# Two heads' scores in one bank, one weighing group per narrow step, and other edits at the ends of the program

## The chip, the cores and the metric

The kernel runs on one core of a Trainium2 chip. The metric is the device time of one execution in microseconds (us). Three runs of the kernel before took 2128.0, 2130.17 and 2129.55 us; the median is 2129.55.

## The reference

The input is x with 2 batches of 1024 tokens and 512 features, in float32. Four residual blocks follow one another:

```
x = x + attention_a(layernorm(x));  x = x + ffn(layernorm(x))
x = x + attention_b(layernorm(x));  x = x + ffn(layernorm(x))
attention: 16 heads of 32, qkv with bias, scores * 32**-0.5, causal mask, softmax, values, output projection with bias
ffn: (silu(h @ w_gate.T) * (h @ w_up.T)) @ w_down.T, hidden size 2048; both ffn blocks share their weights
```

## The kernel before, in words

The program runs four iterations: 2 batches by 2 layers, each an attention and an ffn. Weights and activations are split into a high and a low part (`hi`, `lo`), and each product is three matmuls of type fp32r (`three`, lines 1165 to 1167). Every engine has its own written-out order of work, and semaphores tie them together.

The attention of an iteration is cut into 8 units. Unit u is a group of four heads (u // 2) and a chunk of 512 query tokens (u % 2). `key_tiles(u)` is 4 for an even unit and 8 for an odd one: a unit steps over key tiles j of 128 keys. In each step TensorE computes four transposed score tiles (`scores_t`, line 1256), one for each head, keys by queries, into banks 0 and 1 in turn; ScalarE takes each with one exp into `prob` (`exps`, line 713); in the last four steps of a unit GpSimd masks the diagonal tile of all four heads at once (`mask_probs`, line 605); and TensorE weighs the step before (`weigh`, line 1278): eight matmuls of a 128x32 stationary for the values (the trace has two for each head) and eight for the sums of the exps, into banks 2 and 3. In the last four steps the tiles narrow: `off` leaves 512, 384, 256 and 128 query columns. The order within a step is scores of heads 0 and 1, values, scores of heads 2 and 3, sums, with a place ("point") behind each of the four.

At the points stand the first-pass scores of the next units (`scores`, line 1232, called s1), whose row maxima VectorE takes (`maximum`, line 908), the transposes of the maxima (`mt`, line 1239), and in unit 7 the output projections (`op`) and transposes (`ln2`). `points(u)` computes the places. The maxima, split and negated, go by two small DMAs (`nm_hi`, `nm_lo`) into two more rows of the query stack, and the first transposed score of a unit waits for them.

A unit begins with a head: the q and k projections of unit u + 2 (24 matmuls) in halves, the last weighing of unit u - 1 (`weigh_last`), the scores of step 0, and for units 0, 1, 3 and 5 some early s1 (`BETWEEN`: 2, 1, 2, 1). For the odd units the transpose of their own maxima comes late, in their own head (`MAX_LATE`). ScalarE's order in a head is: evacuate the last unit, the high part of q, the four exps of step 0, the high part of k (line 702). VectorE's order is written out too: the low part of k (line 897) comes ahead of the sixth early s1 (`LO_BEFORE`), and the eight parts of a reciprocal of 512 columns (line 929) lie one behind each s1 from the seventh on.

At the start, VectorE first sets 6144 ones in two rows of the key stacks (line 842), then takes the statistics of the first four token tiles; GpSimd splits the weights of slot 0, then computes the inverse deviation (line 598), then splits slots 1 and 2; VectorE normalises four tiles (line 871), TensorE transposes them, and the value products begin once both value slots are split. At the end, SP stores each of the last batch's eight token tiles and, two tiles later, loads x again into the same place; nothing reads the last four of these.

Of the kernel before, what the change touches and what calls it, by code (L numbers as in the profile page):

```python
# [96 lines left out]

def key_tiles(u):
    return CT * (unit(u)[1] + 1)
# [22 lines left out]

def points(u):

    if u == UNITS - 1:
        return [6, 8, 10, 12, 21, 25]
    if u == UNITS - 2:
        return [0, 2, 4, 6, 10]
    n = len(beside(u)) - sum(BETWEEN.get(u, ()))
    first = FIRST[unit(u)[1]]  # L130
    return [first + i * (4 * (key_tiles(u) - 1) - TAIL - first) // n for i in range(n)]
# [31 lines left out]
LO_BEFORE = {0: (2, 5), 1: (2, 5), 3: (2, 5), 5: (2, 5)}  # L163
RECIPS_FROM = 6
# [17 lines left out]
def block_kernel(nc, x_in, attn_w, ffn_w, qk_bias, row_bias, out):  # L182
    with ExitStack() as ctx:
# [3 lines left out]
        def sem(name):  # L187
# [79 lines left out]
            sem("diff_step"), sem("diff_hi_done"), sem("diff_ready"), sem("s_step"))  # L267

# [142 lines left out]
        def _(sp):  # L411
# [45 lines left out]
            with sp.Fori(0, BATCH) as b:  # L457
# [31 lines left out]
            for s in x_loaded:  # L489
                sp.wait_ge(s, 16 * CT * (BATCH + 1))  # L490
# [7 lines left out]
        def _(pool):  # L498
# [130 lines left out]
            split_weights(0, 0)  # L629
# [49 lines left out]
        def _(act):  # L679
# [11 lines left out]
            def iteration(it):  # L691
# [13 lines left out]
                def exps(u, j, heads):  # L705
                    step = J_BASE[u] + j
                    off = max(0, j - CT * unit(u)[1]) * P
                    if step >= 2:
                        act.wait_ge(pv_done, it * KEY_STEPS + step - 1)
                    for h in heads:  # L710
                        n = GH * step + h
                        act.wait_ge(s2_full, it * S2_STEPS + n + 1)
                        act.activation(prob[:, step % 2, h, off:], bank[n % 2][:, off:], ACT.Exp,  # L713
# [119 lines left out]
            load_table(ACT.Exp)  # L833
            xt_to_hi(0, ("ln1", 0))
# [6 lines left out]
        def _(dve):  # L841
            dve.memset(k_stack[3 * HEAD:3 * HEAD + 2, 1:, :, :].bitcast(F32), 1.0).then_inc(ones_ready, 1)
# [302 lines left out]
        def _(pe):  # L1145
# [13 lines left out]
            def iteration(it):  # L1159
# [15 lines left out]
                def value_part(t, k):  # L1175


                    if k == 0:
# [7 lines left out]
                        pe.wait_ge(w_split, it * SLOTS + V_SLOTS[1] + 1)  # L1186
# [11 lines left out]
                def project(u, w, half):  # L1198

                    g, c = unit(u)  # L1200
                    if half == 0:
# [6 lines left out]
                        if w == 0:  # L1208
# [4 lines left out]
                             for k in range(half * KT // 2, (half + 1) * KT // 2)]  # L1213
                    ins = three(projected(u, w), terms, half == 0, half == 1)
                    if half == 1:
# [26 lines left out]
                def scores_t(u, j, h):  # L1242
# [10 lines left out]
                    if n >= 2:  # L1253
                        pe.wait_ge(prob_ready, it * S2_STEPS + n - 1)
                    rows = slice(0, 3 * HEAD + 2)
                    pe.matmul(bank[n % 2][:, off:], k_stack[rows, keys_of(u, j // CT), h, j % CT * P:(j % CT + 1) * P],  # L1256
# [152 lines left out]
                def project_whole(u, w):  # L1409
                    for half in range(2):  # L1410
                        project(u, w, half)
# [20 lines left out]
                for u in range(UNITS):  # L1432
# [8 lines left out]
                    def between(quarter):  # L1441

                        nonlocal early
                        if u in BETWEEN:
                            for what, *which in beside(u)[early:early + BETWEEN[u][quarter]]:
                                run[what](*which)
                            early += BETWEEN[u][quarter]

                    if u + 2 < UNITS:
                        project(u + 2, 0, 0)  # L1450
                        if u in MAX_LATE:
                            transpose_max(u)
                        weigh_last()
                        between(0)
                        project(u + 2, 0, 1)
                        between(1)
                        scores_t(u, 0, 0)
                        scores_t(u, 0, 1)
                        project(u + 2, 1, 0)
                        between(2)  # L1460
                        scores_t(u, 0, 2)
                        scores_t(u, 0, 3)
                        project(u + 2, 1, 1)
                        between(3)
# [12 lines left out]
                    for j in range(1, key_tiles(u)):  # L1477
                        for half, what in enumerate(("values", "sums")):
                            for own in range(2):
                                if own == 0:  # L1480
                                    scores_t(u, j, 2 * half)
                                    scores_t(u, j, 2 * half + 1)
                                else:
                                    weigh(u, j - 1, what)
                                for (name, *which), at in zip(beside(u)[early:], points(u)):
                                    if at == point and (name != "mt" or which[0] not in MAX_LATE):
                                        run[name](*which)
                                point += 1
# [75 lines left out]
```

## Time and profile before

| | |
|---|---|
| median of 3 runs | 2129.55 us |
| the profiled execution's own time | 2128.06 us |
| its span, first to last instruction | 2126.3 us |
| TensorE busy in the span | 2058.0 us, 97% |
| VectorE, ScalarE, GpSimd busy | 57%, 33%, 47% |
| mean granted TensorE clock | 0.996 |
| VectorE: low part of k (line 897); row maximum (line 908), mean of all | 0.75 us; 0.75 us |
| weight load of TensorE, mean (lines 1256 and 1232) | 0.19 us |
| iteration 2, first transposed score of unit 2 to that of unit 3 | 1175.84 to 1193.58: 17.7 us |
| iteration 2, unit 7, first to last transposed score | 1295.69 to 1327.63: 31.9 us |

The profiled execution took 1.76 us more than its span and 1.49 us less than the median. Its busy time of TensorE counts a matmul from its start to a modelled end, and neighbouring matmuls overlap: a row of 512 columns lasts 390 ns, and the next one starts after some 230 ns. So the pace is read from the starts of the rows, not from their lengths.

### The profile page before, as it was taken

What the parts mean: (1) busy time and instruction counts of PE and PEld (TensorE: products, weight loads), DVE (VectorE), ACT (ScalarE), POOL (GpSimd) and SP (SyncE); (2) the same over time, 40 slices, a digit from 0 to 9 for tenths busy, and PEclk for the clock granted to TensorE, in tenths of its full rate; (3) what the DMA queues carried; (4) which work ended last, traced back from release to release, by engine and by line L of the source; (5) the groups of instructions that cost most, each with busy time, mean ns of one, the idle gap of its engine ahead of it and who ended that gap; (6) DMA issues with size and microseconds to landing.
All of it is one profiled execution on the core that took longest, in us unless ns stands there. A gap on an engine that the chain in (4) does not pass through costs nothing.

```text
span 2126.3 us, 35275 instructions
## 1 busy us (share of the span) xinstructions
PE 2058.0 (97%) x10816; PEld 1442.8 (68%) x10816; DVE 1210.5 (57%) x2452; ACT 698.6 (33%) x1348; POOL 998.0 (47%) x776
## 2 busy tenths in 40 slices
PE   6999999999999999999989999999999999999997
PEld 5555478888755547888765554888887554588886
DVE  6766554455676645544557664555456666444454
ACT  1344432231144443222114444222221444422221
POOL 3323249863312425975331242697533223379752
PEclk9999999999999999999999999999999999999999
DMA  4433101111323200111243320111113232111112
GB/s 130 99 80 82 32 30 50 60 60 40 81 72 81 71 31 30 63 50 58 70 131 72 81 71 32 40 60 50 50 41 83 68 81 71 41 40 60 50 60 89
DMA packets 59756, 135.18 MB, mean 64 GB/s; under 512 B 10784, under 2 KB 11808, under 8 KB 59552
## 3 DMA queue, kind: packets, MB, share of 16 engines
q1 hardware_dynamic: 59552, 132.71, 22.1%
q8 instruction: 98, 1.61, 0.3%
q14 instruction: 106, 0.87, 0.1%
HBM read 77.62 MB, written 4.19 MB: 38 GB/s over the span
## 4 chain that ended last, share of the span: by engine, by line
PE 89%; DVE 3%; issue 3%; ACT 2%; DMA 1%; POOL 1%; SPq 0%; DVEq 0%; POOLq 0%; ACTq 0%
PE bank L1278 13%; PE bank L1165 11%; PE bank L1167 11%; PE bank L1166 11%; PE ring L1165 10%; PE ring L1166 9%; PE ring L1167 9%; PE ring L1232 8%; PE bank L1256 7%; PE ring L1156 1%; ACT prob L713 1%; DMA area<-nm_lo 1%; DVE xn L908 1%; POOL prob L605 1%; DMA x<-x_in 0%
## 5 line engine op out<-in xcount | busy, mean ns | idle before, releaser
L713 ACT ACTIVATE prob<-bank 128x512 f32<-128x512 f32 (+3 forms) x768 | 335.0, 489 | 342.0 <-PE bank L1256 341.2
L908 DVE CUSTOM_DVE_ANT_0 xn<-ring,mask_row 128x128 bf16<-128x128 f32 (+7 forms) x512 | 374.8, 750 | 104.8 <-PE ring L1232 97.8
L605 POOL TENSOR_SCALAR_AFFINE_SELECT prob<-prob 128x512 f32<-128x512 f32 x128 | 83.9, 655 | 567.5 <-ACT prob L713 567.5
L528 POOL TENSOR_SCALAR area<-w_stage 128x1024 fp32r<-128x1024 f32 x131 | 149.8, 1143 | 381.0 <-PE bank L1167 206.7
L530 POOL TENSOR_TENSOR area<-w_stage,area 128x1024 fp32r<-128x1024 f32 x131 | 313.8, 2396 | 10.9
L967 DVE TENSOR_TENSOR x<-x,bank 128x512 f32<-128x512 f32 x256 | 170.8, 685 | 233.2 <-PE bank L1167 233.2
L1165 PE MATMUL ring<-xt_hi,area 128*128 128x512 f32 x688 | 273.8, 398 | 5.2 <-DVE xt_lo L880 2.8
L1166 PE MATMUL ring<-xt_lo,area 128*128 128x512 f32 x688 | 269.4, 392 | 0.0
L1167 PE MATMUL ring<-xt_hi,area 128*128 128x512 f32 x688 | 268.9, 391 | 0.0
L1232 PE MATMUL ring<-area 96*128 96x512 f32 (+3 forms) x768 | 238.8, 372 | 9.5 <-DVE row_max L908 8.5
L1232 PEld LDWEIGHTS ring<-area 96*128 96x128 f32 x768 | 131.0, 188 | 151.0 <-DVE row_max L908 94.6
L1256 PE MATMUL bank<-area 98*128 98x512 f32 (+3 forms) x768 | 225.3, 372 | 7.9 <-DMA area<-nm_lo 4.0
L1256 PEld LDWEIGHTS bank<-area 98*128 98x128 f32 x768 | 125.5, 190 | 122.4 <-ACT prob L713 96.2
L1165 PE MATMUL bank<-area 128*128 128x512 f32 x512 | 200.6, 392 | 2.7 <-DVE area L1035 2.7
L1167 PE MATMUL bank<-area 128*128 128x512 f32 x512 | 199.5, 390 | 0.0
L1166 PE MATMUL bank<-area 128*128 128x512 f32 x512 | 199.5, 390 | 0.0
L1278 PE MATMUL bank<-prob,v 128*32 128x512 f32 (+3 forms) x1536 | 164.4, 500 | 9.1 <-POOL prob L605 7.3
L1278 PE MATMUL bank<-prob,ones 128*32 128x512 f32 (+3 forms) x1536 | 163.2, 497 | 0.0
L1165 PEld LDWEIGHTS ring<-xt_hi,area 128*128 128x128 f32 x688 | 129.6, 188 | 44.2 <-issue 9.8
L1167 PEld LDWEIGHTS ring<-xt_hi,area 128*128 128x128 f32 x688 | 129.7, 189 | 27.7
L1166 PEld LDWEIGHTS ring<-xt_lo,area 128*128 128x128 f32 x688 | 129.9, 189 | 25.5
L929 DVE RECIPROCAL recip<-recip 128x64 f32<-128x64 f32 x256 | 123.8, 522 | 15.0 <-ACT attn L723 15.0
(144 smaller groups left out, 3231.8 us busy)
## 6 DMA issues: line engine op xcount, KB each, us to landing
w_stage<-ffn_w SPq DMA_DIRECT2D x96, 512.0 KB, 3.2
area<-kq_parts SPq DMA_DIRECT2D x336, 128.0 KB, 2.4
w_stage<-attn_w SPq DMA_DIRECT2D x35, 512.0 KB, 3.3
x<-x_in SPq DMA_DIRECT2D x24, 256.0 KB, 3.8
area<-attn SPq DMA_DIRECT2D x48, 128.0 KB, 2.3
out<-x SPq DMA_DIRECT2D x16, 256.0 KB, 2.2
bias_rows<-row_bias SPq DMA_DIRECT2D x10, 256.0 KB, 4.2
area<-nm_hi SPq DMA_DIRECT2D x32, 8.0 KB, 1.8
```

The source lines that it names most:

```text
L528: pool.tensor_scalar(hi, src, 1.0, 0.0, ALU.mult, ALU.add).then_inc(w_hi_done, 1)
L530: pool.tensor_tensor(lo, src, hi.bitcast(F32), ALU.subtract).then_inc(w_split, 1)
L713: act.activation(prob[:, step % 2, h, off:], bank[n % 2][:, off:], ACT.Exp, scale=SCALE).then_inc(prob_ready, 1)
L908: dve.tensor_tensor_reduce(out=sum_out[:, RING[name] % 2, 0:keys], in0=src[:, 0:keys], in1=mask_row[:, TOKENS - keys:], scale=1.0, scalar= ...
L929: dve.reciprocal(recip[:, cols], recip[:, cols]).then_inc(recip_done, 1)
L967: dve.tensor_tensor(x[:, t, :], x[:, t, :], row_bank(s, n)[:, :], ALU.add).then_inc(rows_drained, 1)
L1165: pe.matmul(dst, ah, bh, start=first and k == 0, stop=False, skip_group_check=more)
L1166: pe.matmul(dst, ah, bl, start=False, stop=False, skip_group_check=more)
L1167: ins = pe.matmul(dst, al, bh, start=False, stop=last and k == n - 1, skip_group_check=more)
L1232: ins = pe.matmul(buffer_of(("s1", u, s))[:, kc, 0:n], q, k_stack[0:3 * HEAD, keys_of(u, kc), h, 0:n], start=True, stop=True)
L1256: pe.matmul(bank[n % 2][:, off:], k_stack[rows, keys_of(u, j // CT), h, j % CT * P:(j % CT + 1) * P], q_stack[rows, q_buffer(u), h, off:], ...
L1278: ins = pe.matmul(dst[rows, off:], a, prob[:, step % 2, h, off:], start=j == 0, stop=j == key_tiles(u) - 1, tile_position=(0, h * HEAD))
```

## The change

- `narrow(u, j)` is true in the last two key tiles of a unit (256 and 128 columns). There, `scores_at` puts heads 0 and 1 side by side in bank 0 and heads 2 and 3 in bank 1, ScalarE takes two heads with one exp, and `STEP_PARTS` orders the step as scores of heads 0 and 1, scores of heads 2 and 3, values and sums in one group, nothing. Each of the four parts still has a point behind it. `scores_t` waits for the exps that last read its bank.
- `POINTS` gives the places by hand. `UNIT_START` writes out the head: for even units it is the order of before; for odd units half of the k projection comes ahead of the scores of heads 0 and 1, a quarter behind them and the last quarter behind those of heads 2 and 3. `project` takes a range of its four parts.
- GpSimd sets the ones at the start, and only waits for the four normalised tiles before it subtracts for the low parts of the two value slots; their high parts are made by ScalarE. A value product waits for the slot that it reads.
- SP no longer loads x into the last four tiles of the last batch; the program waits for the stores instead. The batch loop of SP is unrolled.

```diff
+def narrow(u, j):
+    return j >= key_tiles(u) - 2
...
+POINTS = {0: (0, 1, 2, 3, 4, 6, 8, 10, 11), 2: (0, 3, 5, 9, 9), 4: (0, 3, 5, 9, 9),1: (0, 1, 2, 3, 4, 5, 6, 7, 8, 9, 10, 11, 12, 13, 14, 15, 17, 18, 19, 21, 22, 25, 26),6: (0, 2, 4, 5, 10), 7: (4, 8, 10, 12, 21, 25)}
...
+    return POINTS[u if u in POINTS else unit(u)[1]]
...
+STEP_PARTS = (((0,), ("values",), (1,), ("sums",)), ((0,), (1,), ("values", "sums"), ()))
...
+    (("project", 0, range(0, 2)),
+     ("max",),
+     ("last",),
+     ("s1", 2),
+     ("project", 0, range(2, 4)),
+     ("s1", 1),
+     ("project", 1, range(0, 2)),
+     ("scores", 0, 1),
+     ("project", 1, range(2, 3)),
+     ("s1", 2),
+     ("scores", 2, 3),
+     ("project", 1, range(3, 4)),
+     ("s1", 1)))
...
+            if narrow(u, j):
+                n = CHUNK - off
+                return bank[h // 2][:, h % 2 * n:(h % 2 + count) * n]
+            return bank[h % 2][:, off:]
...
-                        if n >= AFTER_STORE:
+                        if n >= AFTER_STORE and not (b == BATCH - 1 and c):
...
+            pool.memset(k_stack[3 * HEAD:3 * HEAD + 2, 1:, :, :].bitcast(F32), 1.0).then_inc(ones_ready, 1)
+            pool.wait_ge(ones_ready, 1)
             inverse_deviation(0, 0, 0)
-            for i in range(1, AHEAD):
+            wait_alone(pool, xn_ready, CT)
+            for i in V_SLOTS:
+                hi, lo = w_part(i, slice(0, SLOT))
+                wait_alone(pool, w_hi_done, i + 1)
+                pool.tensor_tensor(lo, w_stage[:, i, :], hi.bitcast(F32), ALU.subtract).then_inc(w_split, 1)
+            for i in range(len(V_SLOTS), AHEAD):
                 split_weights(0, i)
...
+                    if narrow(u, j):
+                        for h in heads[::2]:
+                            act.wait_ge(s2_full, it * S2_STEPS + GH * step + h + 2)
+                            src = scores_at(u, j, h, 2).rearrange("p (h n) -> p h n", h=2)
+                            act.activation(prob[:, step % 2, h:h + 2, off:], src, ACT.Exp,
+                                           scale=SCALE).then_inc(prob_ready, 2)
+                        return
...
+            for i in V_SLOTS:
+                act.wait_ge(w_loaded[i], 16)
+                act.activation(w_part(i, slice(0, SLOT))[0], w_stage[:, i, :], ACT.Copy).then_inc(w_hi_done, 1)
...
+                    if k % 2 == 0:
+                        pe.wait_ge(w_split, it * SLOTS + V_SLOTS[k // 2] + 1)
...
+                    if narrow(u, j):
+                        pe.wait_ge(prob_ready, it * S2_STEPS + n - h - GH + (GH if h >= 2 else 2 if narrow(u, j - 1) else 3))
+                    elif j == 0 and h < 2 and n >= 2:
+                        pe.wait_ge(prob_ready, it * S2_STEPS + n - h - GH + 2 + 2 * h)
...
```

## Rows read from the trace of the kernel before

**Rows 1.** The page, part 1: busy time, share and instructions of each engine.
```profile
PE 2058.0 (97%) x10816; PEld 1442.8 (68%) x10816; DVE 1210.5 (57%) x2452; ACT 698.6 (33%) x1348; POOL 998.0 (47%) x776
```

**Rows 2.** Waits of TensorE over the span: total us, times, longest.
```profile
PE bank L1278 <- POOL prob L605: 7.3, 20, 0.6
```

**Rows 3.** Timeline of TensorE: start us, us, engine, line, operation (unit 1, iteration 2).
```profile
1171.61 0.64 PE L1278 MATMUL bank<-prob,ones 128*32 128x256 f32 x8
1172.18 0.50 PE L1165 MATMUL ring<-xt_hi,area 128*128 128x512 f32 x1
1172.52 0.40 PE L1166 MATMUL ring<-xt_lo,area 128*128 128x512 f32 x1
1172.75 0.39 PE L1167 MATMUL ring<-xt_hi,area 128*128 128x512 f32 x1
...
1173.44 0.39 PE L1167 MATMUL ring<-xt_hi,area 128*128 128x512 f32 x1
1173.76 0.43 PE L1278 MATMUL bank<-prob,v 128*32 128x128 f32 x8
1174.00 0.40 PE L1278 MATMUL bank<-prob,ones 128*32 128x128 f32 x8
1174.33 0.51 PE L1165 MATMUL ring<-xt_hi,area 128*128 128x512 f32 x1
```

**Rows 4.** Timeline of TensorE, end of unit 7, iteration 3; bracket: idle before.
```profile
1842.68 0.85 PE L1278 MATMUL bank<-prob,v 128*32 128x384 f32 x8 [0.38 <-POOL prob L605]
...
1849.21 0.43 PE L1278 MATMUL bank<-prob,v 128*32 128x128 f32 x8 [0.62 <-POOL prob L605]
```

**Rows 5.** Timeline at the heads of units 1, 3 and 5, iteration 2.
```profile
1140.68 0.72 PE L1256 MATMUL bank<-area 98*128 98x512 f32 x2 [0.68 <-DMA area<-nm_lo]
...
1193.29 0.45 PE L1232 MATMUL ring<-area 96*128 96x384 f32 x1 [0.59 <-DVE row_max L908]
...
1246.84 0.73 PE L1256 MATMUL bank<-area 98*128 98x512 f32 x2 [0.34 <-DMA area<-nm_lo]
```

**Rows 6.** Timeline of ScalarE at the head of unit 1.
```profile
1143.38 1.08 ACT L713 ACTIVATE prob<-bank 128x512 f32<-128x512 f32 x2 [1.09 <-PE bank L1256]
1144.99 0.69 ACT L702 ACTIVATE kq_parts<-ring,bias_qk 128x512 fp32r<-128x512 f32 x1 [0.53 <-PE ring L1167]
```

**Rows 7.** Tile x, first 3 us: transfers issued and their time to landing.
```profile
L448 SPq DMA_DIRECT2D x<-x_in x4: 390/426/432, 0.8 to 2.2; - x4
DMA to landing us min/median/max: 2.7/3.2/4.3
```

**Rows 8.** Timeline of VectorE, the start of the program.
```profile
2.16 5.18 DVE L842 MEMSET area<- 2x6144 f32 x1 [2.16 <-issue]
7.45 2.44 DVE L848 BATCH_NORM_STATS2 stats<-x 128x6 f32<-128x512 f32 x4
12.57 3.75 DVE L871 TENSOR_SCALAR xn<-x,mean_var,rstd 128x512 f32<-128x512 f32 x2 [1.14 <-POOL rstd L598]
...
31.24 1.00 DVE L871 TENSOR_SCALAR xn<-x,mean_var,rstd 128x512 f32<-128x512 f32 x2 [0.49 <-POOL rstd L598]
```

**Rows 9.** Timeline of TensorE, the start.
```profile
16.46 1.94 PE L1156 MATMUL ring<-ident,xn 128*128 128x128 f32 x8 [16.46 <-DVE xn L871]
...
21.71 0.78 PE L1165 MATMUL ring<-area,xt_hi 128*128 128x512 f32 x1
```

**Rows 10.** Groups of GpSimd by line: busy us, mean ns.
```profile
L530 POOL TENSOR_TENSOR area<-w_stage,area 128x1024 fp32r<-128x1024 f32 x131 | 313.8, 2396 | 10.9
L671 POOL MEMSET area<- 2x6144 f32 x4 | 20.9, 5229 | 0.5
```

**Rows 11.** Timeline of the SP queue, end of the program.
```profile
2119.34 0.33 SPq L484 DMA_DIRECT2D out<-x  x1
2119.83 3.15 SPq L488 DMA_DIRECT2D x<-x_in  x3
```

**Rows 12.** Busy time and granted clock in one stretch of unit 7, iteration 1.
```profile
769.30:772.70 3.40, 3.40 (x14) 0.71 (x10) 0.00 (x0) 1.54 (x4) 3.14 (x4) 0.50 0.00 0
```

More of the change, by code:

```diff
@@ L163 @@
 LO_BEFORE = {0: (2, 5), 1: (2, 5), 3: (2, 5), 5: (2, 5)}
+STEP_PARTS = (((0,), ("values",), (1,), ("sums",)), ((0,), (1,), ("values", "sums"), ()))
+UNIT_START = (
+    (("project", 0, range(0, 2)),
[7 more added lines that the diff above has]
+     ("scores", 2, 3),
+     ("project", 1, range(2, 4)),
+     ("s1", 1)),
+    (("project", 0, range(0, 2)),
+     ("max",),
+     ("last",),
+     ("s1", 2),
+     ("project", 0, range(2, 4)),
+     ("s1", 1),
+     ("project", 1, range(0, 2)),
+     ("scores", 0, 1),
+     ("project", 1, range(2, 3)),
+     ("s1", 2),
+     ("scores", 2, 3),
+     ("project", 1, range(3, 4)),
+     ("s1", 1)))
 RECIPS_FROM = 6
@@ L456, in _ @@
                 load_weights(i, None, attn_w[0])
-            with sp.Fori(0, BATCH) as b:
+            for b in range(BATCH):
                 with sp.Fori(0, LAYERS) as layer:
@@ L1212, in project @@
                     terms = [(*w_part(QK_SLOT0 + g, slice((2 * k + w) * P, (2 * k + w + 1) * P)), *xt_part(k, cols))
-                             for k in range(half * KT // 2, (half + 1) * KT // 2)]
-                    ins = three(projected(u, w), terms, half == 0, half == 1)
-                    if half == 1:
+                             for k in ks]
+                    ins = three(projected(u, w), terms, ks[0] == 0, ks[-1] == KT - 1)
+                    if ks[-1] == KT - 1:
                         ins.then_inc(side_full if u in SIDE_UNITS else ring_full, 1)
@@ L1409, in project_whole @@
                 def project_whole(u, w):
-                    for half in range(2):
-                        project(u, w, half)
+                    project(u, w, range(KT))
                 for t in range(CT - 1):
@@ L1439, in iteration, with between @@
                     early = 0
-                    def between(quarter):
+                    def between(count):
                         nonlocal early
[L1444 to L1447, printed above, removed]
+                        for what, *which in beside(u)[early:early + count]:
+                            run[what](*which)
+                        early += count
                     if u + 2 < UNITS:
[L1450 to L1464, printed above, removed]
+                        for what, *which in UNIT_START[unit(u)[1]]:
+                            if what == "project":
+                                project(u + 2, *which)
+                            elif what == "max" and u in MAX_LATE:
+                                transpose_max(u)
+                            elif what == "last":
+                                weigh_last()
+                            elif what == "scores":
+                                for h in which:
+                                    scores_t(u, 0, h)
+                            elif what == "s1" and u in BETWEEN:
+                                between(*which)
                     else:
@@ L1477, in iteration @@
                     for j in range(1, key_tiles(u)):
[L1478 to L1482, printed above, removed]
+                        for part in STEP_PARTS[narrow(u, j)]:
+                            for what in part:
+                                if what in (0, 1):
+                                    scores_t(u, j, 2 * what)
+                                    scores_t(u, j, 2 * what + 1)
                                 else:
                                     weigh(u, j - 1, what)
[L1485 to L1488, printed above, removed]
+                            for (name, *which), at in zip(beside(u)[early:], points(u)):
+                                if at == point and (name != "mt" or which[0] not in MAX_LATE):
+                                    run[name](*which)
+                            point += 1
                 weigh(UNITS - 1, key_tiles(UNITS - 1) - 1, "values")
```

32 lines of the change are left out of this document (13 added, 19 removed).

## The prediction

> **What bounds the kernel now.** I read the page's busy shares first, then TensorE's waits, then the timeline at the places that the change touches. TensorE is busy for 97% of the span and no other engine for more than 57% [rows 1], so time goes down only where TensorE does less, waits less, or starts earlier, or where the program ends sooner after it. The reader is to see that little of the gain can be in recorded waits: those on GpSimd's mask, the largest inside the iterations, are 7.3 us in all [rows 2]. What the change removes is mostly inside "busy", and only the starts of the rows show it.
>
> **1. Merged weighing.** Take the starts in [rows 3]. Plain products follow each other in 0.23 us (1172.52 to 1172.75). A product followed by a weighing group takes 0.32 (1173.44 to 1173.76): 0.09 to go in. The 128-column values go over to the sums in 0.24, the sums to a product in 0.33: 0.09 to come out, and none between values and sums. The first product behind a group takes 0.34 (1172.18 to 1172.52) where others take 0.23: 0.11 more, which I read as a weight load that could not run ahead. So a separate group costs 0.18 us for the two changes, and up to 0.29 with the load.
> The new order takes out one group in each narrow step: 2 steps x 8 units x 4 iterations = 64. Unit 7 is in part 2; 56 are left. Where s1 still stands beside the scores the whole 0.29 goes; where four short score tiles now come together, weight loads bind them and part of it stays. Ends: 56 x 0.18 = 10.1 and 56 x 0.29 = 16.2 us. I take 0.26, nearer the upper end since in the odd units s1 stands at four of the eight narrow points: 14.6 us. The paired exps take time from ScalarE alone, which is off the path; a pair must wait for its second head's matmul, but its reader comes a whole group later.
> The Trainium skill, "TensorEngine Tiling (Array Packing)", section "Tiling Modes", says that a change of tiling mode drains the engine. It names only the drain, so by it alone this part would be the lower end, some 4.5 us less than I take; the 0.34 behind a group in [rows 3] says that there is more to a change than the two drains.
>
> **2. The end of unit 7.** Nothing but transposes fills its last steps, and three values groups stand for the mask; the first and last idle 0.38 and 0.62 us [rows 4]. Before, the exps of heads 2 and 3 come between values and sums, and the mask behind them is late. In the new order they come a whole group (1.0 to 1.4 us) and eight transposes earlier, so mask and exps are done. Walking the new order from 1841.79: two pairs of 256 columns 0.45, transposes 0.9, values and sums of 384 columns 4 x 0.33 + 0.2; two pairs of 128 columns 0.5, transposes 0.9, 8 groups of four matmuls of 256 columns at 0.22, then the last weighing without a stall, 0.55. The first product of the output projection stands at about 1848.1, where the last weighing of before [rows 4] ends at 1849.2 + 0.57 = 1849.8. That is 1.7 us, both merges counted: 6.8 in four iterations. Ends: the merges alone, 0.5 each, 2.0; and 1.9 each, 7.6.
>
> **3. Heads of the odd units.** The first transposed score of unit 1 idles 0.68 us for the maxima's DMA and that of unit 5 0.34; in unit 3 the wait is before, on VectorE (0.59), and stays [rows 5]. By starts the two are worth 0.8 and 0.6. Six products (1.36 us) now stand ahead of those scores, so these stalls go. But what is late next? ScalarE must still do two exps (1.08) and the high part of k (0.69) [rows 6], then VectorE the low part (0.75) and one row maximum (mean 0.75, for one of 256 columns some 0.4; both in the table above), before the eighth s1 has its buffer; with the scores of heads 2 and 3 followed by only three products instead of six, and an s1 at each of points 0 and 1 where only point 1 had one, TensorE reaches that s1 some 0.4 us too early, in all three units. 4 x (0.8 + 0.6 + 0.05) = 5.8 gained, 12 x 0.4 = 4.8 lost. I take a gain of 1.0; ends: a gain of 5.8, a loss of 5.
> The other moved points cost nothing in my account: in units 1, 3 and 5 all s1 come earlier or at the same distance, so that VectorE has more room at the narrow end. The output projection in unit 7 moves from point 6 to 4; its input was split about 0.9 us before that point, and if it were late the price would be under 1 us an iteration.
>
> **4. The start.** Four tiles of x are issued by 2.2 and the last takes up to 4.3 [rows 7]: in place at 6.5. VectorE starts on them only at 7.45, behind its 5.18 us of ones, which go to GpSimd (5.23 there [rows 10]) and end by 8.1. So statistics start 0.9 earlier. The inverse deviation then finds GpSimd idle instead of in a subtraction (2.4 [rows 10]). And two normalised tiles take 3.75 us [rows 8] while GpSimd splits weights, but 1.00 when it does not. My walk: statistics 6.55 to 9.6, inverse deviation to 10.7, four tiles to 12.7, high and low parts of the first pair to 16.3, when the first value product starts; it was at 21.71 [rows 9]. Low part of slot 0 is there at 15.2, of slot 1 at 17.6, both in time. 5.4 us earlier; TensorE runs the first stretch at the slower pace and has more of its products in it, for which I take off 0.4. Gain 5.0, ends 4.0 and 5.4; slot 2 comes at 22.2 where it is read at some 26, so the lead is kept.
> The Trainium skill, "SBUF — State Buffer", section "Who interferes with whom", says that GpSimd shares a port pair with some VectorE instructions and that the one issued second blocks. The 3.75 against 1.00 agrees. By the same rule the ones, if still being written when VectorE's first such instruction is issued, would hold it; they end a microsecond earlier, so the sum stays.
>
> **5. The end.** The last store is issued at 2119.34, held by the order of stores and loads, and three loads end the program [rows 11]: the span ends 2126.3. Without them the last store goes out at about 2118.6, lands 2.2 to 3.2 later and the program ends 0.5 behind it: 2121.3 to 2122.3. Gain 4.6, ends 4.0 and 5.0.
>
> **Sum.** 14.6 + 6.8 + 1.0 + 5.0 + 4.6 = 32.0. The profiled execution's own time is 2128.06: 2096.1. The median of the runs stood 1.5 above it; the profiled execution itself holds stretches at the lower of TensorE's two levels (granted 0.50, that is 1.2 GHz, in 3.4 us of unit 7 [rows 12]), and such things vary by run. I forecast 2097.5.
>
> **Rivals.**
> A. *Only the drains go.* Scores of narrow tiles come in fours, and their weight loads take back what the group's end gave. For it: a weight load lasts 0.19 us (the table), and 128 columns stream in a quarter of the 0.23 that 512 take. Against it: pairs of 128 columns were so bound before. Then 10.1 + 4.0 - 4.0 + 5.0 + 4.6 = 19.7: 2109.9 on the median's scale. The skill's rule on draining points here. Chance 0.14.
> B. *Heads pay fully and nothing new is late.* If VectorE's lead is longer than my walk says, part 3 gives 5.8; with the upper ends of part 1 the sum is 38.4: 2091. For it: VectorE is busy for 57% only. Chance 0.18.
> C. *The start is handed back.* The projections wait for slot 2, or VectorE for the second four tiles, whose times hang on loads and not on TensorE. Then 27: 2102.5. Against it: 4 us of slack above. Chance 0.08.
> D. *Slower.* The heads of the odd units become a chain: scores of heads 2 and 3, two exps, high part of k, low part of k, maximum, 0.3 + 1.08 + 0.69 + 0.75 + 0.4 = 3.2 us, with nothing beside it. 12 x 3.2 = 38 against 31: 2136. It decides from 2.6 us a head on. Against it: between those scores and the s1 that waits stand some 2.6 us of TensorE's own work. Chance 0.04.
> The forecast has 0.56.
>
> **Range and chances.** The lower ends of all parts give 2129.5 - 15 = 2114, the upper ones 2129.5 - 40 = 2089.5. I give 2089 to 2109, which takes in A's edge and B. A change of under 0.2% (4 us) could not be told from none here. Slower by more: D, 0.04. Within: 0.03, where A, C and half of D come together. Faster: 0.93.
>
> **What would show it.** Right: in the last two steps of a unit the weighing rows stand as 16 matmuls in a line, and a unit 2 or 4 takes 0.5 us less from first score to first score (17.7 before, the table); no mask waits at the end of unit 7, which is 1.7 us shorter; first transposes near 11.9 and first value product near 16.3; the last transfer is a store. Wrong: s1 waits on VectorE at the second point of units 1, 3 and 5 longer than 0.5 us, pairs of narrow scores start more than 0.3 us apart, or a new wait on the weights of slot 2 at some 26 us. The forecast falls if the iterations after the first give less than 3 us each.

## The result, and the profile after

The changed kernel takes 2079.24 us (median of 5 runs, 2076.52 to 2083.13) against 2129.55: a ratio of 0.9765, 95% interval 0.9749 to 0.9781. The forecast was 2097.5 with a range of 2089 to 2109, so the sign was right and the gain of 50 us was larger than the range allows.

The profiled execution took 2079.24 us itself, with a span of 2077.5 us against 2126.3. The page of the changed kernel gives each engine's busy us, share of the span and instructions:

```profile
PE 2033.5 (98%) x10816; PEld 1444.8 (70%) x10816; DVE 1197.3 (58%) x2451; ACT 688.0 (33%) x1222; POOL 999.9 (48%) x775
```

Its waits of TensorE: total us, times, longest.

```profile
PE ring L1286 <- DVE row_max L961: 5.5, 16, 0.6
...
PE bank L1314 <- ACT prob L764: 3.7, 12, 0.5
...
PE bank L1336 <- POOL prob L643: 0.7, 4, 0.2
```

TensorE's instructions are as many as before [rows 1] and 24.5 us of its busy time are gone; the other half of the 48.8 us by which the span is shorter was idle time. GpSimd's mask is waited for 4 times in place of 20 [rows 2], and the maxima's DMA has no row at all; in the kernel before it had this one:

```profile
PE bank L1256 <- DMA area<-nm_lo: 4.0, 8, 0.7
```

Where the 48.8 us lie, from the starts of rows in the two traces (first and last transposed score of each iteration, last matmul, end of span):

| stretch | before | after | gain | forecast |
|---|---|---|---|---|
| start of the span to the first transposed score | 68.80 | 61.80 | 7.0 | 5.0 |
| four attentions, first to last transposed score | 835.3 | 797.2 | 38.1 | |
| last transposed score to the next iteration's first, three times, and to the last matmul | 1210.7 | 1212.4 | -1.7 | |
| the two rows above, parts 1 to 3 | | | 36.4 | 22.4 |
| last matmul to the end of the span | 11.47 | 6.06 | 5.4 | 4.6 |

Every part gave more than its term, and the iterations hold 14 of the missing 17 us. An attention without a stretch at half clock takes 198.9 to 199.0 us in place of 208.4 to 208.5.

The narrow steps at the end of unit 1, iteration 2, in the trace of the changed kernel (start us, us, engine, line, operation), which answer to [rows 3]:

```profile
1104.89 0.34 PE L1314 MATMUL bank<-area 98*128 98x128 f32 x2
...
1105.52 0.34 PE L1314 MATMUL bank<-area 98*128 98x128 f32 x2
1105.79 0.64 PE L1336 MATMUL bank<-prob,v 128*32 128x256 f32 x8
1106.25 0.61 PE L1336 MATMUL bank<-prob,ones 128*32 128x256 f32 x8
1106.79 0.74 PE L1286 MATMUL ring<-area 96*128 96x512 f32 x2
```

Values and sums are one line of 16 matmuls, one change in and one out. The end of unit 7, which answers to [rows 4]: no bracket, thus no wait, at the last two steps, and the last weighing 0.9 us behind the first of its group.

```profile
1803.34 0.66 PE L1314 MATMUL bank<-area 98*128 98x128 f32 x4
1803.84 1.06 PE L1209 MATMUL ring<-ident,attn 128*128 128x128 f32 x8
1804.83 0.64 PE L1336 MATMUL bank<-prob,v 128*32 128x256 f32 x8
1805.28 0.61 PE L1336 MATMUL bank<-prob,ones 128*32 128x256 f32 x8
1805.72 0.40 PE L1336 MATMUL bank<-prob,v 128*32 128x128 f32 x8
```

The head of unit 1, which answers to the first row of [rows 5]: six more products stand between s1 and the first transposed score, and no wait is recorded.

```profile
1111.66 0.34 PE L1286 MATMUL ring<-area 96*128 96x384 f32 x1
1111.83 0.40 PE L1218 MATMUL ring<-xt_hi,area 128*128 128x512 f32 x1
...
1112.98 0.39 PE L1220 MATMUL ring<-xt_hi,area 128*128 128x512 f32 x1
1113.21 0.63 PE L1314 MATMUL bank<-area 98*128 98x512 f32 x2
...
1116.00 0.79 PE L1314 MATMUL bank<-area 98*128 98x512 f32 x2
1116.62 0.34 PE L1286 MATMUL ring<-area 96*128 96x384 f32 x1
1116.90 1.07 PE L1336 MATMUL bank<-prob,v 128*32 128x512 f32 x8
1117.99 0.50 PE L1286 MATMUL ring<-area 96*128 96x512 f32 x1
```

The start on VectorE, against [rows 8]: a pair of normalised tiles takes 1.00 us.

```profile
10.62 1.00 DVE L924 TENSOR_SCALAR xn<-x,mean_var,rstd 128x512 f32<-128x512 f32 x2 [1.22 <-POOL rstd L636]
```

The start on TensorE, against [rows 9]: the first product stands at 16.33, and the next follows in 0.33 and then in 0.23.

```profile
11.77 1.94 PE L1209 MATMUL ring<-ident,xn 128*128 128x128 f32 x8 [11.77 <-DVE xn L924]
13.50 1.80 PE L1209 MATMUL ring<-ident,attn 128*128 128x128 f32 x8
16.33 0.49 PE L1218 MATMUL ring<-area,xt_hi 128*128 128x512 f32 x1 [1.03 <-DVE xt_lo L933]
16.66 0.40 PE L1219 MATMUL ring<-area,xt_hi 128*128 128x512 f32 x1
```

The end on the SP queue, against [rows 11]: four stores, no load behind them.

```profile
2072.73 2.12 SPq L520 DMA_DIRECT2D out<-x  x4
```

Both profiles hold two stretches of 3.4 us at about half the granted clock (1.2 of 2.4 GHz); this is the one of unit 7, iteration 2, as in [rows 12]. That unit took 30.91 us from first to last score where the other three took 29.35, so it cost 1.56 us. Both kernels have one in an attention and one between two attentions, so the difference above holds none.

```profile
1264.50:1267.90 3.40, 3.40 (x14) 0.70 (x10) 0.00 (x0) 1.44 (x3) 3.21 (x4) 0.52 0.00 0
```

### The profile page after: what moved, and what is told of

Same layout as the page of the kernel before. It is cut to its first block, busy times and chain, and to the rows that moved or that the text cites. A ratio compares the mean times of both kernels' runs of the same rounds, so it can differ in the third digit from the quotient of the medians.

```text
span 2077.5 us, 34948 instructions
## 1 busy us (share of the span) xinstructions
PE 2033.5 (98%) x10816; PEld 1444.8 (70%) x10816; DVE 1197.3 (58%) x2451; ACT 688.0 (33%) x1222; POOL 999.9 (48%) x775
## 4 chain that ended last, share of the span: by engine, by line
PE 92%; DVE 3%; issue 3%; ACT 1%; DMA 1%; POOL 0%; DVEq 0%; SPq 0%; POOLq 0%; ACTq 0%
PE bank L1336 13%; PE bank L1218 11%; PE bank L1220 11%; PE bank L1219 10%; PE ring L1218 10%; PE ring L1220 9%; PE ring L1219 9%; PE ring L1286 9%; PE bank L1314 7%; PE ring L1209 1%; DVE xn L961 1%; DMA x<-x_in 0%; ACT prob L764 0%; DVE stats L901 0%; PE ring L1293 0%
## 5 line engine op out<-in xcount | busy, mean ns | idle before, releaser
L764 ACT ACTIVATE prob<-bank 128x512 f32<-128x512 f32 (+1 forms) x512 | 264.4, 570 | 214.8 <-PE bank L1314 214.0
L568 POOL TENSOR_TENSOR area<-w_stage,area 128x1024 fp32r<-128x1024 f32 x129 | 309.1, 2396 | 10.8
L1314 PE MATMUL bank<-area 98*128 98x512 f32 (+3 forms) x768 | 212.1, 365 | 3.9 <-ACT prob L764 3.7
```

Source lines behind the costliest of these rows:

```text
L568: pool.tensor_tensor(lo, src, hi.bitcast(F32), ALU.subtract).then_inc(w_split, 1)
L764: act.activation(prob[:, step % 2, h, off:], scores_at(u, j, h), ACT.Exp, scale=SCALE).then_inc(prob_ready, 1)
L1314: pe.matmul(scores_at(u, j, h), k_stack[rows, keys_of(u, j // CT), h, j % CT * P:(j % CT + 1) * P], q_stack[rows, q_buffer(u), h, off:], s ...
```

## Experiments

"Steps" are the merged order, packing, paired exps and the relaxed waits on exps; "places" is the new table of points. Kernels of one group ran on one chip; each was timed beside the kernel before, whose medians there were 2127.59, 2129.35 and 2129.29 us. The changed kernel was not timed again beside them, so "slower than the changed kernel" compares with the 2079.24 above, whose own kernel before stood at 2129.55. There is one profile of each kernel.

### One part added to the kernel before

**The end alone.**

```diff
-                        if n >= AFTER_STORE:
+                        if n >= AFTER_STORE and not (b == BATCH - 1 and c):
...
```

> The kernel before with the edit at the end of the program alone (no last four loads of x, waits for the stores). If the end is worth what the two traces show between the last matmul and the end of the span (11.4 us before, 6.1 after), the time is 5.4 us below the kernel before. By the term of my forecast it is 4.6, at most 5.0.

2122.58 us, ratio 0.9973 (0.9962 to 0.9985): 5.0 us. Its last matmul starts at 2114.22 and the span ends at 2120.3: 6.1 us, as in the changed kernel.

**The start alone**: ones on GpSimd, value slots split by ScalarE and GpSimd behind the four normalised tiles.

> The kernel before with the edits at the start alone. If the 6.8 us by which the first transposed score comes earlier are the start's own, the time is 6.8 us below the kernel before, and the first value product runs at 0.23 us at once. By my forecast 5.0, at most 5.4, with the first products at 0.43 us for some 4 us.

2121.38 us, ratio 0.9969 (0.9959 to 0.9979): 6.2 us. The first transposed score stands at 63.89, 4.9 us earlier than before and 2.1 later than in the changed kernel. The transposes and the first product stand within 0.05 us of their places there. What differs is the pace behind them; these are its first products:

```profile
16.38 0.79 PE L1174 MATMUL ring<-area,xt_hi 128*128 128x512 f32 x1 [0.92 <-DVE xt_lo L889]
16.96 0.63 PE L1175 MATMUL ring<-area,xt_hi 128*128 128x512 f32 x1
17.39 0.63 PE L1176 MATMUL ring<-area,xt_lo 128*128 128x512 f32 x1
17.81 0.63 PE L1174 MATMUL ring<-area,xt_hi 128*128 128x512 f32 x1
```

They follow each other in 0.43 us, until 20.8, where the changed kernel's follow in 0.23 from the second on. The granted clock is 1.00 in both. So the forecast's 5.0 fits an execution that starts slowly, as the profile of the kernel before does too, and 2.1 of the 7.0 above lie in the pace. The new start comes with both paces: of the eight profiles in this document that hold it, three start at 0.23 and five at 0.43. So I put the 2.1 down to the execution and not to the edit; no kernel was profiled twice to show it.

**The steps alone**, at the old places, with the old heads.

```diff
...
+STEP_PARTS = (((0,), ("values",), (1,), ("sums",)), ((0,), (1,), ("values", "sums"), ()))
```

> The kernel before with the narrow steps alone: paired scores and exps, values and sums in one group, the relaxed waits; the places of s1, the heads, the start and the end are those of before. If one merged group is worth 0.33 us: 64 x 0.33 = 21, and 5 to 9 more for the end of unit 7 and the mask that comes earlier, 26 to 30 us below. By my forecast's terms 14.6 + 6.8 = 21.4, at most 23.8.

2124.4 us, ratio 0.9987 (0.9976 to 0.9997): 3.2 us, where parts 1 and 2 of the forecast sum to 21.4 and I expected 26 to 30. Merging pays here too (the last two steps of unit 2, up to the projection, take 4.57 us where the kernel before takes 5.20), but TensorE now waits for VectorE's maxima 48 times, and for the maxima's DMA longer:

```profile
PE ring L1279 <- DVE row_max L955: 17.9, 48, 0.6
PE bank L1307 <- DMA area<-nm_lo: 6.6, 12, 0.9
```

**The heads alone**: half of the k projection ahead of an odd unit's first scores.

```diff
+     ("project", 1, range(0, 2)),
      ("scores", 0, 1),
-     ("project", 1, range(0, 2)),
+     ("project", 1, range(2, 3)),
      ("s1", 2),
      ("scores", 2, 3),
-     ("project", 1, range(2, 4)),
+     ("project", 1, range(3, 4)),
```

> The kernel before with the heads of units 1, 3 and 5 in the new order alone. If the stalls on the maxima's DMA go and little comes back: 0.8 and 0.6 an iteration less at most 0.3, 4 to 5 us below. By my forecast 1.0 us below (5.8 gained, 4.8 lost on the eighth s1).

2121.29 us, ratio 0.9968 (0.9956 to 0.9979): 6.3 us. An undisturbed attention takes 207.02 us, 1.4 less than before, no waits for the maxima's DMA are left, and waits for row maxima do not grow (7.9 us, 20 times). The forecast's loss of 4.8 at the eighth s1 is not there; but the old places, which this kernel keeps, put no s1 at point 0.

### One part taken out of the changed kernel

**Values and sums apart again** (packing and places stay).

```diff
-STEP_PARTS = (((0,), ("values",), (1,), ("sums",)), ((0,), (1,), ("values", "sums"), ()))
+STEP_PARTS = (((0,), ("values",), (1,), ("sums",)), ((0,), ("values",), (1,), ("sums",)))
```

> The changed kernel with values and sums apart again in the narrow steps (order of before, packed scores and pair exps kept). If a merged group is worth 0.33 us by itself: 64 x 0.33 = 21 slower than the changed kernel, some 25 with the masks at the end of unit 7. By my forecast's price 0.26: 17. If the gain came from the packing or the places of s1 instead: less than 8 slower.

2117.97 us, ratio to before 0.9944 (0.9923 to 0.9965): 38.7 us slower than the changed kernel, more than twice the 14.6 + 2.0 that the groups themselves were to cost and more than the 25 expected. The mask is late:

```profile
PE bank L1336 <- POOL prob L643: 11.0, 28, 0.7
```

That is 10.3 us of it. The last two steps of unit 2 take 5.50 us here, more than the 5.20 of the kernel before: packed scores with the groups apart are worse than either kernel, so the 38.7 is not what merging is worth against the kernel before.

**The old places** under everything else.

```diff
-    return POINTS[u if u in POINTS else unit(u)[1]]
...
+    first = FIRST[unit(u)[1]]
+    return [first + i * (4 * (key_tiles(u) - 1) - TAIL - first) // n for i in range(n)]
```

> The changed kernel with the places of s1 of before. The theory after x3_steps: the merged narrow steps shorten TensorE's part of a step, and with the old places VectorE's row maxima bind there, so that the gain is handed to s1 waits. Then it is 18 to 25 us slower than the changed kernel, with 40 or more waits of s1 on row maxima (16 in the changed kernel). If the places are worth nothing by themselves, as my forecast had it: within 3 us of the changed kernel.

2104.94 us, ratio 0.9888 (0.9869 to 0.9907): 25.7 us slower. Its waits for row maxima are those of the steps alone, 17.9 us in 48 times against 5.5 in 16, which is half of it; the rest stands in no recorded wait. TensorE at the end of unit 1: four s1 stand in a line, and the next ones wait for VectorE, with only packed scores between.

```profile
1118.56 1.03 PE L1292 MATMUL ring<-area 96*128 96x512 f32 x4
1119.42 0.34 PE L1320 MATMUL bank<-area 98*128 98x128 f32 x2
1120.35 0.73 PE L1292 MATMUL ring<-area 96*128 96x512 f32 x2 [0.59 <-DVE row_max L967]
```

**The old heads** under everything else (the diff of the heads, reversed).

> The changed kernel with the odd heads in the order of before. If the head is worth in company what it was alone (5.7 us by its trace): 5 to 7 slower than the changed kernel, with eight waits on the maxima's DMA back. If VectorE is later there with the new places: more, 8 to 10. By my forecast 1.0.

2092.3 us, ratio 0.9827 (0.9808 to 0.9847): 13.1 us slower, twice what the heads gave alone and more than the 10 expected. The maxima's DMA is waited for 12 times:

```profile
PE bank L1313 <- DMA area<-nm_lo: 9.9, 12, 1.3
```

**No packing**: the merged order stays (by a function of its own), heads take banks 0 and 1 in turn again, with one exp each, and each score waits again for the exp of the score two before it.

```diff
 def narrow(u, j):
-    return j >= key_tiles(u) - 2
+    return False
...
-                        for part in STEP_PARTS[narrow(u, j)]:
+                        for part in STEP_PARTS[short(u, j)]:
```

> The changed kernel with the merged order in the narrow steps, but each head's scores in banks 0 and 1 in turn and one exp for each head. The scores of heads 2 and 3 must then wait for the exps of heads 0 and 1 of their own step. If packing is what lets the group be merged, 128 such waits of 0.2 to 0.4 us, partly behind an s1: 15 to 35 us slower than the changed kernel. If packing is only ScalarE's saving and off the path: within 3 us.

2116.68 us, ratio 0.9941 (0.9923 to 0.996): 37.4 us slower. The scores of heads 2 and 3 now follow those of heads 0 and 1 into the same banks and must wait for their exps:

```profile
PE bank L1317 <- ACT prob L769: 19.4, 64, 0.5
```

In the changed kernel such waits are 3.7 us in 12 times, so the record names 15.7 of the 37.4. Packing is what lets the merged order pay, not an extra of ScalarE's.

### Steps and places together, places alone, and two more

The eight kernels left open whether steps and places by themselves account for the iterations.

> The kernel before with two edits together, the narrow steps (packed, merged, relaxed waits) and the new places, but its old heads, start and end. Theory (steps and places need each other): alone the steps gave 5 us and the places are worth 22 us only where the steps are merged, so the two together give what the changed kernel keeps beyond its heads, start and end: 26 to 31 us, 2099 to 2104, attention of an iteration about 202 us (208.4 before), waits for row maxima down from 17.9 us to about 8, none on GpSimd's mask over 1 us in all. Rival of the prediction's account (places cost and give nothing, steps 14.6 + 6.8 = 21.4): about 2108, and attention 203 us. Rival that effects only add up by single edits (5 us from the steps, nothing from places): 2124.

2107.62 us, ratio 0.99 (0.988 to 0.992): 21.7 us. An undisturbed attention takes 202.1 us, as the theory had it, but part is handed on behind its last score, and four stretches at half clock stand in the profile where the kernel before has two. The theory of 2099 to 2104 failed; the forecast's sum for parts 1 and 2, 21.4, is met. The heads, not the steps, hold what is missing. TensorE at the heads of units 1, 3 and 5 of iteration 2 here:

```profile
1128.00 0.34 PE L1273 MATMUL ring<-area 96*128 96x384 f32 x1
1129.38 0.72 PE L1301 MATMUL bank<-area 98*128 98x512 f32 x2 [1.04 <-DMA area<-nm_lo]
...
1181.34 0.72 PE L1301 MATMUL bank<-area 98*128 98x512 f32 x2 [0.83 <-DMA area<-nm_lo]
...
1233.17 0.72 PE L1301 MATMUL bank<-area 98*128 98x512 f32 x2 [0.34 <-DMA area<-nm_lo]
```

Against [rows 5], unit 1's wait has grown from 0.68 to 1.04, and unit 3 has one of 0.83 where it had none.

**The places alone** in the kernel before.

> The kernel before with the new places alone; steps, heads, start and end as before. Theory (the places pay only beside merged steps): with values and sums apart, the places that the merged steps leave between scores and weighing fall elsewhere, the narrow steps lose cover, and waits for exps or the mask grow: between 3 us faster and 10 us slower than before, 2126 to 2140, attention 208 to 211 us an iteration. Rival (the places themselves carry the 22 us, by giving VectorE room): 2107, attention 203 us. Rival (places are worth nothing by themselves, as in the prediction): within 2 us of before.

2134.34 us, ratio 1.0026 (1.0016 to 1.0036): 5.1 us slower. Waits for the mask grow from 7.3 us [rows 2]:

```profile
PE bank L1275 <- POOL prob L602: 10.2, 32, 0.6
```

The four corners, as gain against the kernel before on the same chip:

| | old places | new places |
|---|---|---|
| old steps | 0 | -5.1 |
| new steps | 3.2 | 21.7 |

21.7 - 3.2 + 5.1 = 23.6 us belong to neither alone. So it is only beside the steps that the places cost nothing, as the forecast had it.

**GpSimd subtracts without waiting** for the normalised tiles.

```diff
-            wait_alone(pool, xn_ready, CT)
```

> The changed kernel, in which GpSimd no longer waits for the four normalised tiles before it subtracts for the low parts of the value slots. Theory (GpSimd's subtractions slow VectorE's normalise, 3.75 us for two tiles in the kernel before against 1.00 without them): the normalise rows take 2 to 4 us a pair again, the first product stands 1 to 4 us later than 16.33, and the products behind it start at the slower pace for longer if the transposes have gaps; first transposed score at 64 to 67 (62.0 in the changed kernel), median 2081 to 2085. Rival (no contention between the two here; the 3.75 came from something else): normalise rows 1.0 us, the same first score or up to 1 us earlier, median 2078 to 2080.

2086.93 us, ratio 0.9805 (0.9786 to 0.9823): 7.7 us slower than the changed kernel. VectorE at the start of this kernel:

```profile
11.08 5.04 DVE L923 TENSOR_SCALAR xn<-x,mean_var,rstd 128x512 f32<-128x512 f32 x2 [1.22 <-POOL rstd L636]
16.03 0.99 DVE L923 TENSOR_SCALAR attn<-x,mean_var,rstd 128x512 f32<-128x512 f32 x2
```

GpSimd, the same stretch:

```profile
11.01 4.82 POOL L674 TENSOR_TENSOR area<-w_stage,area 128x1024 fp32r<-128x1024 f32 x2
```

While GpSimd works (11.01 to 15.83) VectorE needs 5.04 us for two tiles, behind it 0.99. The first theory holds, but its price was too low: the first product stands at 20.82, 4.5 us later, where at most 4 were expected, and the median is above the 2085 of its upper end. The pace behind the product is 0.23 in both, and the first score stands at 66.26, 4.5 us later too. Most of the other 2.6 us of span lie in the change from the first batch to the second (321.77 against 318.85 us from score to score); that stretch varies from 317.0 to 322.3 over the kernels here, and what sets it was not looked into.

**The merged order in every step**, packing still in the last two alone.

```diff
-STEP_PARTS = (((0,), ("values",), (1,), ("sums",)), ((0,), (1,), ("values", "sums"), ()))
+STEP_PARTS = 2 * (((0,), (1,), ("values", "sums"), ()),)
```

> The changed kernel with the merged order (scores of heads 0 and 1, scores of heads 2 and 3, values and sums as one group) in every key tile of every unit; packing and paired exps stay in the last two. It takes out one more weighing group in 32 steps an iteration, 128 in all. Theory 1 (a removed group is worth 0.33 us also in wide steps, where exps have a step's time): 128 x 0.2 to 0.33 = 26 to 42 us faster than the changed kernel, 2037 to 2053. Theory 2 (in wide steps banks are the limit: scores of the next step need the bank whose exp comes last, with nothing between the two pairs of scores but s1 places, so TensorE waits for ScalarE's exps at 0.54 us each): waits on exps of 0.3 to 1.0 us a step, 10 to 60 us slower, 2090 to 2140. I hold theory 2, since each bank serves two heads in turn and four exps of 512 columns take 2.2 us.

2152.04 us, ratio 1.0111 (1.0091 to 1.0131): 72.8 us slower than the changed kernel, though 128 groups fewer change in and out. I held the second theory; its place was right, its upper bound too low. Waits on exps and on row maxima:

```profile
PE bank L1314 <- ACT prob L764: 23.5, 65, 0.6
PE ring L1286 <- DVE row_max L961: 22.9, 52, 1.0
```

Against the changed kernel's 3.7 and 5.5 these two rows hold 37 of the 72.8 us.

## Why the prediction was wrong

**Part 3, the heads, is the step that failed: 1.0 forecast, 13.4 found.** The steps and places together take 23.0 us off the iterations and the heads, added last, 13.4: four attentions take 833.8 us before, 808.4 with steps and places and 795.7 in the changed kernel, each without its half-clock stretches (one, three and one at 1.55 us), and the stretches between them and to the last matmul give 2.3 back and take 0.7 off again. The medians agree: 13.1 for taking the heads out. Added first, the heads give 6.3, also above the 5.8 of the term's upper end; the 7 us between the two figures belong to heads, steps and places together. Two things were wrong in the term.

*The loss.* "TensorE reaches that s1 some 0.4 us too early, in all three units" was to cost 4.8 us. ScalarE's and VectorE's chain is as long as I had it: from the scores of heads 2 and 3 (1114.67) to the end of the maximum that, by the forecast, the eighth s1 needs it takes 3.26 us, where rival D has 3.2. Its last link, on VectorE in the changed kernel:

```profile
1117.52 0.41 DVE L961 CUSTOM_DVE_ANT_0 xn<-ring,mask_row 128x256 bf16<-128x256 f32 x1
```

What was wrong is TensorE's side. The eighth s1 stands 1.09 us behind the values ahead of it (1116.90 to 1117.99, the head of unit 1 above), where 1.00 is usual: 0.1 us and not 0.4. Another 0.15 falls one place earlier, where I had looked for nothing: the first two scores of the next step take 0.62 us (1116.00 to 1116.62) against 0.47 with the old heads, since the exp of head 3 ends at 1116.24 and holds the bank of the second. Together 0.25 a head, 3.0 us in place of 4.8.

*The gain.* I priced the stalls as the trace of before had them, 0.8 + 0.6 us (and 0.05 that no row shows), and left out unit 3. The chain that has to be covered starts inside the head, at the transpose of the maxima, and goes through VectorE and two DMAs to the first score. From that transpose to that score, over the twelve heads of a profile:

| kernel | sum | shortest, longest | low part's DMA landed after |
|---|---|---|---|
| before | 44.1 | 3.65, 3.70 | 3.53 to 3.57 |
| steps alone | 44.4 | 3.64, 3.87 | 3.52 to 3.75 |
| places alone | 44.3 | 3.65, 3.73 | 3.53 to 3.56 |
| steps and places | 47.5 | 3.65, 4.39 | 3.53 to 4.27 |
| changed, with 16.6 us of products more | 53.3 | 4.25, 4.55 | 3.53 to 4.30 |

Two readings follow. First, unit 3 is bound by the same 3.7 us as the others: the maxima's DMA landed 3.54 us behind the transpose there as well, hidden behind the wait on VectorE, and the six products cover it too. Second, with steps and places both in, the chain itself is longer in some heads, because the issue of the last DMA takes longer. Unit 1, iteration 2, kernel before:

```profile
1138.71 0.59 SPq L444 DMA_DIRECT2D area<-nm_lo  x1
```

The same with steps and places:

```profile
1127.02 0.98 SPq L479 DMA_DIRECT2D area<-nm_lo  x1
```

That makes 3.3 us which neither edit brings alone and which the new heads cover; what slows the issue stays open. Nor did the "VectorE (0.59), and stays" in unit 3 stay: no wait is recorded there in the changed kernel, and by starts 0.2 us of it is left. With the heads alone unit 3 still takes 5.08 us from transpose to score, in the changed kernel 4.53, which is 2.2 us in four iterations. The normalise of VectorE in unit 3's head, iteration 2, kernel before, and what GpSimd does beside it:

```profile
1191.79 1.24 DVE L935 TENSOR_TENSOR attn<-attn,recip 128x512 f32<-128x512 f32 x1
1190.10 2.38 POOL L530 TENSOR_TENSOR area<-w_stage,area 128x1024 fp32r<-128x1024 f32 x1
```

The same instructions in the changed kernel:

```profile
1161.55 0.69 DVE L988 TENSOR_TENSOR attn<-attn,recip 128x512 f32<-128x512 f32 x1
1159.10 2.37 POOL L568 TENSOR_TENSOR area<-w_stage,area 128x1024 fp32r<-128x1024 f32 x1
```

Before, GpSimd's subtraction of weights runs until 1192.48, over the normalise; now it ends at 1161.47, just ahead of it. It comes earlier since the mask ahead of it does (0.8 us before the head's first product, where it started together with it). Six kernels agree: where the subtraction runs over the normalise by 0, 0.45, 0.45, 0.70, 0.70 and 0.83 us (changed, old places, steps alone, before, heads alone, groups apart), it takes 0.69, 1.00, 1.00, 1.24, 1.25 and 1.38, and no mask runs beside it in any. At the start the same pair of engines gave 5.04 against 0.99. An edit of the subtraction's place alone was not tried.

From the last weighing to the second weighing group of the next unit, the twelve heads take 125.8 us before and 120.1 with the heads alone, 130.8 with steps and places and 119.9 in the changed kernel (in the last two the new places put one s1 more into this stretch). So 10.9 of the 13.4 us lie in the heads; the remaining 2.5 I did not place.

**Parts 1 and 2, the steps: 21.4 forecast, 21.7 by the medians, 23.0 by the traces.** The size is right and its make-up is not. A merged group is worth more than 0.26: the last two steps of unit 2, up to the projection and with as many s1 in them, went from 5.20 to 4.53 us, 0.33 for each group. If all 56 are worth that, they give 18.5. Unit 7, from its first score to the first product of the output projection, went from 33.98 to 31.89 us (2.6 less up to its last score, 0.5 handed on), four times 2.1 or 8.4, above the 7.6 of the term's upper end: 26.9 in all. Against that stand the 3.3 us of longer waits in the heads. My walk through unit 7 was also added up wrongly: its items make 6.6 us, not the 6.3 that 1848.1 stands for, and the 1.76 in it for the weighing of 256 columns was 0.89 (1804.83 to 1805.72). Rival A, only the drains, is excluded: four packed scores of 128 columns start 0.11 to 0.16 us apart, where a quarter of 0.23 would be 0.06, so something like A's weight loads does bind them, and the 0.33 is what is left after that. The Trainium skill's rule ("TensorEngine Tiling (Array Packing)", section "Tiling Modes") is right as far as it goes: the two drains of 0.09 are in the rows, but they are little over half of what a group costs.
One sign that I named is not met: from the first score of unit 2 to that of unit 3 was to take 0.5 us less than 17.7, and takes 17.98. I had overlooked that part 3 moves 1.38 us of products into this stretch; with the steps alone it takes 17.04 to 17.25.
"The other moved points cost nothing in my account" stood on the count of s1 alone and was right by luck of the pairing: without the new places 18.5 of the 21.7 us are lost again, beside 48 waits for row maxima, and the places without the steps lose 5.1. The output projection's move from point 6 to 4 showed no new wait.

**Part 4, the start: 5.0 forecast, 7.0 in the profile, 4.9 and 6.2 alone (trace, medians).** Every place was right within 0.2 us: transposes 11.77 for 11.9, first product 16.33 for 16.3. Some of that is luck: in four other kernels with the same start these stand at 12.5 to 12.7 and at 17.1 to 17.2. The faster pace behind the first product was worth 2.1 here. The Trainium skill's rule on port pairs ("SBUF — State Buffer", section "Who interferes with whom"), by which the engine that issues second waits, fits the 5.04 and 0.99 above: GpSimd was 0.07 us ahead.

Rival C, a start that is handed back, did not come: no matmul waits for a weight slot.

**Part 5, the end: 4.6 forecast, 5.4 in the profile, 5.0 alone.** The last store was to be issued at about 2118.6; with the end alone, where the last matmul starts 0.6 us earlier than before, the last four are issued together from 2115.53 on, within 2.12 us, so by 2117.7.

**The rivals and the range.** B had the mechanism of the heads and was still 12 us short; D's chain has the length that D gave it, but runs beside TensorE's own work. The four errors had one sign (12.4, 1.6, 2.0 and 0.8 us). The upper ends of the parts summed to 40, and the one that was furthest off, part 3's 5.8, was bounded by the stalls of before. A bound that is read from a trace holds only while the other edits leave its chain as it is.

## What to carry to other kernels

Before pricing an edit that covers a wait, measure the whole chain behind it, from the instruction that starts it to the one that waits, in every place where it occurs: another wait can hide it (unit 3), and other edits can lengthen it (44.1 to 47.5 us here), so its stalls in the trace of before are no upper bound. Price edits that share a buffer, an order or a stretch of time as a pair: here steps and places gave 3.2 and -5.1 us alone and 21.7 together, and packing, merging and places each cost 26 to 39 us when taken out.

## What the runs showed of the hardware

- The first products of an execution may run at 0.43 us each (until 19.9 to 26.1 us) or at 0.23 at once, with a granted clock of 1.00 in both; the same transposes with the same gap of 0.9 to 1.0 us stand ahead in either case (16.38 in the kernel with the start alone, 16.33 in the changed one). It is worth 2.1 us; what decides it stays open.
- Ahead of the last matmul, stretches at half the granted clock come one to five times in a profile. Most last 3.4 us and cost some 1.55 each: two in the changed kernel, four with steps and places at the old heads (mean clock 0.995 or 0.996 in each of its four runs). Some last 6.8 us: one each in three kernels, and three of the five with the merged order everywhere. Why these have more stays open.
- Two tiles of a VectorE normalise take 1.0 us alone and 3.75 to 5.04 beside GpSimd's subtractions; the multiply of two operands took 1.24 beside one such subtraction against 0.69 behind it.
